# A graph layer on one core: when GpSimd may refill a slot of the ring of gathered rows

## The chip, the core and the metric

The kernel runs on one core of one Trainium2 chip. The metric is the device time of one execution in microseconds (us). TensorE is written PE, VectorE DVE, ScalarE ACT, GpSimd POOL and SyncE SP, as in the profile.

## What is computed

The input is a graph of 2500 nodes with 256 features each and 80000 edges, sorted by destination. The part of the reference that this change touches is the attention over the edges:

```
xl = (xn @ W_l).reshape(N, 4, 64);  xr = (xn @ W_r).reshape(N, 4, 64)
e = xl[src] + xr[dst];  e = where(e >= 0, e, 0.2 * e)
score = einsum('ehd,hd->eh', e, att)
ex = exp(score - segment_max(score, dst)[dst])
agg = segment_sum(ex / segment_sum(ex, dst)[dst] * xl[src], dst)
```

After it come an ELU, a layer norm and a residual, and a sum with a second branch (a lambda layer: a softmax over the nodes, a 256x256 context, a product with queries). Last there is a mixture of eight experts with a capacity, of which each node takes one.

## The kernel before

`graph_block` runs four stages one after the other: `survey` (norms, the tables xl and xr, tables for the edges), `attend` (the attention), `node_update` and `experts`. Only `attend` changes.

The edges are cut into 704 groups of up to 128 edges, and 4 groups make a **quad**: there are `QUADS` = 176 of them. Every engine goes through the quads in the same order with its own instruction stream, and semaphores alone bind the engines together. Eight quads (`RUN`) are a run, since the maxima of the segments are found once for each run. `over_quads` writes the first turn of 16 quads out, then loops nine times over a turn of 16, and writes the last turn out with the steps that follow it. I call the piece of an engine's stream for quad q **its step q**.

- **POOL**, step q: four indirect DMAs at L1080, one for each group. Each fetches 128 rows of `d_xl` (260 floats, 1040 bytes) by source node into `gathered_rows`. This tile is a ring with `RING` = 16 slots of one quad. Slot q % 16 was last used by quad q - 16, so the first two gathers of quad q wait until ACT has made the first half of the products of quad q - 16 (`prod`, two counts for each quad), and the other two wait for the second half. The gathers of quads 0 to 7 are issued by `survey`. Those of quads 8 to 15 stand in the first turn and have nothing to wait for.
- **SP**, step q: loads for quad q into rings of four, `e_drow` (L1014) and `e_xr` (L1015), and the store of the sums (L1030).
- **PE**, step q: `edges(q)`, 12 matmuls that pick rows of xr (L1400), and two that add the gathered rows of groups 0 and 1 by the identity (L1405, 4 in the profile's count); before the first of these PE waits for all four gathers of quad q. The rows of groups 2 and 3 are added by DVE. Behind it in the same stream stands `sums(q - 12)` (L1454), which needs the products of quad q - 12.
- **DVE**, step q: `sum_edges(q)` (L1154), which waits for `edges(q)`, for the gathers of quad q and for an older score; then the mask for quad q + 2 (L1146), two leaky parts (L1160, L1164), the sums of quad q - 13 (L1193), a mask for quad q - 10 (L1179), and `scores(q)` (L1171). In the first five steps of a run there are small operations for the segment maxima too. In the first turn DVE, PE and ACT also do the lambda branch: `keys_less` (L1112), `contexts` (L1346) and others. POOL has one operation of it (L228), behind the gathers of quad 15.
- **ACT**, step q: `weights(q - 11)`, an exponential (L1505) and 16 scaled copies (L1509), the products. It waits for `sums(q - 13)`, which PE does in its step q - 1.

So a gather for quad q is released by products made in ACT's step q - 5, and read by PE and DVE in their step q.

Of the kernel before, what the change touches and what calls it, by code (L numbers as in the profile page):

```python
# [38 lines left out]
RING = 2 * RUN  # L39
# [21 lines left out]
BLANKS = 2 * (TURNS - 2)  # L61
BLANK = -(-(TRASH + 1) // (2 * BLANKS)) * 2
EARLY = RING // 2
LN_EPS = 1e-5
CONSTANTS = 20 * 16


def settle(eng, m):


    eng.sem_inc(m.met, 1)
# [28 lines left out]
def sem_set(nc, ctx, prefix, names):  # L100

    sems = {}
    for name in names.split():
        if name[-1] == "*":
            sems[name[:-1]] = [semaphore(nc, ctx, f"{prefix}_{name[:-1]}{i}") for i in range(2)]
        else:
            sems[name] = semaphore(nc, ctx, f"{prefix}_{name}")
    return sems
# [91 lines left out]
def ring_view(m, half, partitions, *shape, dt=F32):  # L200
# [5 lines left out]
    m.used[half] += n  # L206
    assert m.used[half] <= EARLY * G * ROW
    flat = m.ring[:, half * EARLY * G:(half + 1) * EARLY * G, :].rearrange("p n c -> p (n c)")
    view = flat[0:partitions, at:at + n]
# [16 lines left out]
def rstd_pool(pool, out, var, halves):  # L226

    return pool.tensor_tensor(out, var, halves, ALU.pow)  # L228


def survey(nc, ctx, m, a):
# [104 lines left out]
    with nc.Block() as block:  # L336
# [64 lines left out]
        def _(pool):  # L401
# [10 lines left out]
            def first_rows():  # L412
# [3 lines left out]
                settle(pool, m)  # L416
                for i in range(EARLY * G):
                    pool.indirect_dma_start(m.ring[:, i, :], None, m.d_xl, bass.IndirectOffsetOnAxis(
# [42 lines left out]
        def _(dve):  # L461
            ch = Chain(dve, s["chain"], 0)

            def variances(b):
# [7 lines left out]
                dve.wait_ge(s["norm"], 8 * b + 8)  # L472
                dve.tensor_scalar(ve[:, 4 * b:4 * b + 4], mv[:, 4 * b:4 * b + 4, 1], LN_EPS, None, ALU.add).then_inc(s["var"], 1)

# [451 lines left out]
def over_quads(eng, body, behind=0):  # L926

    for slot in range(RING):
        body(Quad(0, slot))
    with eng.Fori(1, TURNS - 1) as turn:  # L930
        for slot in range(RING):
            body(Quad(turn, slot))
    for slot in range(RING + behind):
        body(Quad(TURNS - 1, slot))


def attend(nc, ctx, m, a):
# [3 lines left out]
    s = sem_set(nc, m.sems, "att", "init idx sel edges summed relu score lin turned run top ends heads fwd bwd carried drop cols raised tops topped diff rr f fac ex prod selt agg old acc rows* links fixed shares")  # L941
# [8 lines left out]
    score = sb("e_score", [P, 2, HEADS, SUBS_RUN])  # L950
# [16 lines left out]
    prod = sb("e_prod", [P, 2, G, HEADS, HCOLS])  # L967
# [35 lines left out]
    with nc.Block() as block:  # L1003
# [61 lines left out]
        @block.gpsimd  # L1065
        def _(pool):
            def quad(q):
                p = q.slot // RUN
                if q.at == 0 and not q.known():
                    pool.wait_ge(s["idx"], q.run - 1)  # L1070
                if q.known() and q.k < EARLY:
                    return
                for g in range(G):
                    if g % 2 == 0 and q.since(RING):
                        pool.wait_ge(s["prod"], (q.k - RING) * 2 + g // 2 + 1)
                    if g % 2 == 0:
                        settle(pool, m)
                    at = q.at * G + g
                    column = m.idx[:, q.k * G + g:q.k * G + g + 1] if q.known() else idx[p][:, at:at + 1]
                    pool.indirect_dma_start(xl[:, q.slot * G + g, :], None, m.d_xl, bass.IndirectOffsetOnAxis(  # L1080
                        ap=column, axis=0)).then_inc(gathered[q.slot], 16)
                if q.known() and q.k == RING - 1:
                    pool.wait_ge(sl["var"], 2)
                    rstd_pool(pool, rs[:, :], ve[:, :], neghalf[:, :]).then_inc(sl["rstd"], 1)
            over_quads(pool, quad)
            pool.wait_ge(sl["mix"], 2)
            pool.tensor_tensor(m.b_mix[:, :], m.b_mix[:, :], m.beta[:, :], ALU.add).then_inc(sl["rowed"], 1)
            pool.wait_ge(sl["rowed"], 1)
            pool.wait_ge(sl["x"], 16 * (FOURS + 1))
            for b in range(FOURS):  # L1090
                four = m.x[:, 4 * b:4 * b + 4, :]
                pool.tensor_tensor(four, four, m.b_mix[:, :].unsqueeze(1).to_broadcast([P, 4, DIM]), ALU.add)

        @block.vector
        def _(dve):
# [23 lines left out]
            def lambda_rows():  # L1119
# [5 lines left out]
                for half in range(2):  # L1125
# [3 lines left out]
                    lamed.step(dve.bn_aggr(mv[:, half, :], st[:, half, :]))  # L1129
                dve.tensor_scalar(ve[:, :], mv[:, :, 1], LN_EPS, None, ALU.add).then_inc(sl["var"], 1)  # L1130

# [427 lines left out]
def node_update(nc, ctx, m, a):  # L1559
# [54 lines left out]
    with nc.Block() as block:  # L1614
# [90 lines left out]
        def _(dve):  # L1705
# [75 lines left out]
            def first_stats(b):  # L1781
# [8 lines left out]
                dve.wait_ge(s["aggr1"], 4 * b + 4)  # L1790
                dve.tensor_scalar(ve1[:, tiles], mv1[:, tiles, 1], LN_EPS, None, ALU.add).then_inc(s["var1"], 1)

            def residual(b):
# [19 lines left out]
                dve.wait_ge(s["aggr2"], 4 * b + 4)  # L1813
                dve.tensor_scalar(ve2[:, tiles], mv2[:, tiles, 1], LN_EPS, None, ALU.add).then_inc(s["var2"], 1)

# [306 lines left out]
```

## Time and profile before

| what | value |
|---|---|
| median of the runs | 1652.13 us |
| lowest, highest of 3 runs | 1651.43, 1689.13 us |
| the profiled execution | 1662.86 us, its span 1661.1 us |
| PE, DVE, ACT, POOL busy, share of the span | 73%, 65%, 51%, 49% |
| granted clock of PE, mean | 0.871 |
| gathers at L1080 | 672 |

The profile is one execution. Its times count from the start of its span; what lies around the span is 1.8 us. The busy time of a POOL gather is the time in which POOL writes it out for the DMA engines, not that of the transfer. "Idle before" is the time in which the engine did nothing ahead of an instruction, and the name behind it what ended it ("remote": an update that the records do not tie to an instruction; "issue": nothing that the profile shows).

### The profile page before, as it was taken

What the parts mean: (1) busy time and instruction counts of PE and PEld (TensorE: products, weight loads), DVE (VectorE), ACT (ScalarE), POOL (GpSimd) and SP (SyncE); (2) the same over time, 40 slices, a digit from 0 to 9 for tenths busy, and PEclk for the clock granted to TensorE, in tenths of its full rate; (3) what the DMA queues carried; (4) which work ended last, traced back from release to release, by engine and by line L of the source; (5) the groups of instructions that cost most, each with busy time, mean ns of one, the idle gap of its engine ahead of it and who ended that gap; (6) DMA issues with size and microseconds to landing.
All of it is one profiled execution on the core that took longest, in us unless ns stands there. A gap on an engine that the chain in (4) does not pass through costs nothing. (4 is left out here: it accounts for less than half of the span.)

```text
span 1661.1 us, 24931 instructions
## 1 busy us (share of the span) xinstructions
PE 1217.6 (73%) x5659; PEld 865.7 (52%) x5659; DVE 1082.3 (65%) x2307; ACT 848.9 (51%) x3252; POOL 816.1 (49%) x849
## 2 busy tenths in 40 slices
PE   6754877767877677777877777867767747399995
PEld 4322755555555555555655555645545536355663
DVE  7442876776776666776778676866767858404444
ACT  3220176656666576657666675756656823132221
POOL 5625055555555555456555565556546154502223
PEclk9866998889898899878889998988989977589997
DMA  6544256555566556566565655656755125334340
GB/s 181 147 150 113 67 142 167 147 161 153 161 169 155 146 159 166 147 166 162 160 161 163 164 164 152 172 151 162 210 147 155 40 65 165 123 120 140 102 127 17
DMA packets 167498, 237.47 MB, mean 143 GB/s; under 512 B 40113, under 2 KB 134018, under 8 KB 167407
## 3 DMA queue, kind: packets, MB, share of 16 engines
q1 hardware_dynamic: 123310, 130.22, 26.9%
q0 software_dynamic: 41216, 103.67, 24.2%
q10 hardware_dynamic: 2880, 2.66, 0.5%
q14 instruction: 72, 0.58, 0.1%
q8 instruction: 20, 0.33, 0.1%
HBM read 189.57 MB, written 48.91 MB: 144 GB/s over the span
## 5 line engine op out<-in xcount | busy, mean ns | idle before, releaser
L1080 POOL DMA_INDIRECT gathered_rows<-d_xl,e_idx x576 | 547.3, 950 | 425.2 <-ACT e_prod L1509 180.6
L1509 ACT ACTIVATE e_prod<-gathered_rows,e_prod 128x64 f32<-128x64 f32 x2728 | 679.1, 335 | 46.4 <-issue 39.6
L1454 PE MATMUL bank<-e_prod,e_selt 128*128 128x260 f32 x1408 | 402.4, 432 | 133.8 <-DMA gathered_rows<-in_src_dram,n_row_of 58.7
L1454 PEld LDWEIGHTS bank<-e_prod,e_selt 128*128 128x128 f32 x1408 | 286.0, 211 | 229.0 <-issue 82.9
L1400 PE MATMUL bank<-e_xr,e_sel 128*128 128x256 bf16 x2112 | 327.2, 293 | 54.0 <-issue 38.5
L1154 DVE TENSOR_TENSOR e_edge<-bank,gathered_rows 128x512 f32<-128x512 f32 x176 | 119.7, 680 | 279.2 <-remote 241.7
L1400 PEld LDWEIGHTS bank<-e_xr,e_sel 128*128 128x128 bf16 x2112 | 217.4, 105 | 154.3 <-issue 81.8
L1405 PE MATMUL bank<-gathered_rows,ident 128*128 128x256 f32 x704 | 233.6, 411 | 36.2 <-issue 36.0
L1171 DVE TENSOR_REDUCE e_score<-e_edge 128x16 f32<-128x1024 f32 x176 | 212.8, 1209 | 0.3
L1505 ACT ACTIVATE e_prod<-e_diff 128x16 f32<-128x16 f32 x176 | 39.4, 224 | 203.6 <-remote 121.6
L1405 PEld LDWEIGHTS bank<-gathered_rows,ident 128*128 128x128 f32 x704 | 118.6, 210 | 39.4 <-issue 33.1
L1080 POOL DMA_INDIRECT gathered_rows<-d_xl,src_cols x96 | 90.7, 945 | 88.1 <-ACT e_prod L1509 29.9
L1179 DVE TENSOR_TENSOR e_selt<-bank,cyclic_cols 128x512 f32<-128x512 f32 x176 | 119.6, 680 | 11.0 <-PE bank L1454 7.2
L1949 POOL DMA_INDIRECT out_dram<-f_out,f_index x32 | 45.3, 1417 | 159.2 <-DVE f_out L2064 154.3
L1160 DVE SCALAR_TENSOR_TENSOR e_edge<-bank,att_relu 128x512 f32<-128x512 f32 x176 | 119.4, 678 | 0.0
L1164 DVE SCALAR_TENSOR_TENSOR e_edge<-e_edge,bank 128x512 f32<-128x512 f32 x176 | 118.5, 673 | 0.0
L1971 PE MATMUL bank<-f_rowst,w_rows 128*128 128x391 f32 x256 | 87.5, 500 | 0.7 <-ACT f_rowst L2012 0.7
L1193 DVE SCALAR_TENSOR_TENSOR e_acc<-e_acc,keep_cols,bank 128x260 f32<-128x260 f32 x154 | 73.4, 476 | 21.4 <-remote 12.5
L1983 PE MATMUL bank<-f_hid,w_rows 128*128 128x391 f32 x256 | 85.8, 492 | 0.0
L1498 ACT ACTIVATE e_rr<-e_drop 1x4 f32<-1x4 f32 x22 | 4.5, 204 | 151.2 <-DVE e_drop L1251 119.1
L1971 PEld LDWEIGHTS bank<-f_rowst,w_rows 128*128 128x128 f32 x256 | 49.3, 193 | 37.4 <-issue 2.7
L1422 PE MATMUL bank<-ident,e_top 128*1 128x128 f32 x22 | 7.1, 322 | 83.7 <-DVE e_top L1221 58.4
(315 smaller groups left out, 1165.0 us busy)
## 6 DMA issues: line engine op xcount, KB each, us to landing
e_xr<-d_xr SPq DMA_DIRECT2D x176, 192.0 KB
d_hist<-e_acc SPq DMA_DIRECT2D x176, 130.0 KB
e_drow<-d_rel SPq DMA_DIRECT2D x176, 128.0 KB
w_rows<-in_L_ffn_w_dram SPq DMA_DIRECT2D x16, 1024.0 KB, 7.2
gathered_rows<-d_xl,e_idx POOLq DMA_INDIRECT x576
d_in<-lambda_w SPq DMA_DIRECT2D x18, 350.7 KB
e_rows<-d_rows SPq DMA_DIRECT2D x22, 192.5 KB
x_rows<-in_x_dram SPq DMA_DIRECT2D x8, 512.0 KB, 5.5
```

What stands on the lines that cost most here:

```text
L1080: pool.indirect_dma_start(xl[:, q.slot * G + g, :], None, m.d_xl, bass.IndirectOffsetOnAxis(ap=column, axis=0)).then_inc(gathered[q.slot], 16)
L1154: dve.tensor_tensor(edge[:, b, 2:4, :], ps_edge[b][1][:, :].rearrange("p (g c) -> p g c", g=2), xl[:, q.slot * G + 2:q.slot * G + 4, 0:DIM ...
L1160: dve.scalar_tensor_tensor(out=edge[:, b, 0:2, :], in0=ps_edge[b][0][:, :].rearrange("p (g c) -> p g c", g=2), scalar=0.0, in1=m.att_relu[ ...
L1164: dve.scalar_tensor_tensor(out=edge[:, b, 2:4, :], in0=edge[:, b, 2:4, :], scalar=0.0, in1=att_relu.unsqueeze(1).to_broadcast([P, 2, DIM]) ...
L1171: dve.tensor_reduce(score[:, p, :, q.at * G:q.at * G + G].rearrange("p h g -> p g h"), edge[:, b, :, :].rearrange("p g (h c) -> p g h c", ...
L1179: dve.tensor_tensor(selt[:, b, :, :], lane_up.unsqueeze(1).to_broadcast([P, G, P]), m.cyclic[:, bass.ds(q.k * G, G)].unsqueeze(2).to_broad ...
L1400: last = pe.matmul(out, sel[:, b, g * P:g * P + P], xr[:, r, part * DIM:part * DIM + DIM], start=(part == 0), stop=(part == 2 and g >= 2))
L1405: last = pe.matmul(out, m.ident[:, :], xl[:, q.slot * G + g, 0:DIM], start=False, stop=True)
L1454: last = pe.matmul(ps_agg[b], selt[:, b, g, :], flat(prod[:, b, g, :, :]), start=(g == 0), stop=(g == G - 1))
L1509: last = act.activation(prod[:, b, g, h, 0:HEAD], xl[:, q.slot * G + g, h * HEAD:h * HEAD + HEAD], ACT.Copy, scale=prod[:, b, g, h, HEAD:H ...
L1971: last = pe.matmul(m.bank[2 + f % 2][:, 0:CAP], w1[:, q, half, f * P:f * P + P], rowst[:, q, half, :], start=(half == 0), stop=(half == 1))
L1983: last = pe.matmul(m.bank[4 + to][:, 0:CAP], w2[:, q, f, to * P:to * P + P], hid[:, f, :], start=(f == 0), stop=(f == FCH - 1))
```

## The change

A constant `LEAD` = 13 is added. From quad 16 on, the gathers of quad q wait for the products of quad q - 13 in place of quad q - 16. In the first turn, the gathers of quads 8 to 15 wait until the scores of quad q - 8 (`EARLY` = 8) are written. Nothing else changes: the ring keeps its 16 slots, and every gather, matmul and load stays.

```diff
+LEAD = 13
...
                 for g in range(G):
                     if g % 2 == 0 and q.since(RING):
-                        pool.wait_ge(s["prod"], (q.k - RING) * 2 + g // 2 + 1)
+                        pool.wait_ge(s["prod"], (q.k - LEAD) * 2 + g // 2 + 1)
+                    elif g == 0:
+                        pool.wait_ge(s["score"], q.k - EARLY + 1)
                     if g % 2 == 0:
                         settle(pool, m)
```

## Rows read from the trace of the kernel before

**Rows 1.** Busy time by stretch: stretch, length, engines, PE clock, DMA share, GB/s

```profile
117.00:162.00 45.00, 18.31 (x77) 11.31 (x77) 11.35 (x20) 2.11 (x2) 30.26 (x32) 0.65 0.43 115
...
211.00:1286.00 1075.00, 796.70 (x4015) 587.41 (x4016) 764.49 (x1468) 681.55 (x2809) 610.99 (x643) 0.89 0.59 160
```

**Rows 2.** Groups by line, DVE from 211 to 1286 us: busy, mean ns, idle before

```profile
L1154 DVE TENSOR_TENSOR e_edge<-bank,gathered_rows 128x512 f32<-128x512 f32 x161 | 109.4, 680 | 240.7 <-remote 212.4 <-PE bank L1405 20.5 <-issue 7.8
```

**Rows 3.** The waits: who for whom, total us, times, longest

```profile
POOL gathered_rows L1080 <- ACT e_prod L1509: 210.5, 79, 10.8
```

**Rows 4.** Timeline of POOL, first turn: start, duration, what, idle before

```profile
117.24 0.94 POOL L1080 DMA_INDIRECT gathered_rows<-d_xl,src_cols  x1 [29.20 <-POOLq L2096]
...
156.00 0.95 POOL L1080 DMA_INDIRECT gathered_rows<-d_xl,src_cols  x1 [0.30 <-issue]
198.97 0.85 POOL L228 TENSOR_TENSOR l_rs<-l_ve,l_neghalf 128x2 f32<-128x2 f32 x1 [42.03 <-DVE l_ve L1130]
210.59 1.02 POOL L1080 DMA_INDIRECT gathered_rows<-d_xl,e_idx  x1 [10.76 <-ACT e_prod L1509]
```

**Rows 5.** Timeline of DVE, quads 0 to 3

```profile
123.86 0.69 DVE L1154 TENSOR_TENSOR e_edge<-bank,gathered_rows 128x512 f32<-128x512 f32 x1 [4.32 <-issue]
...
134.10 0.69 DVE L1154 TENSOR_TENSOR e_edge<-bank,gathered_rows 128x512 f32<-128x512 f32 x1 [5.71 <-remote]
...
162.13 0.69 DVE L1154 TENSOR_TENSOR e_edge<-bank,gathered_rows 128x512 f32<-128x512 f32 x1 [23.49 <-remote]
...
166.58 0.68 DVE L1154 TENSOR_TENSOR e_edge<-bank,gathered_rows 128x512 f32<-128x512 f32 x1
```

**Rows 6.** Timeline of PE, first turn

```profile
138.30 0.28 PE L1400 MATMUL bank<-e_xr,e_sel 128*128 128x256 bf16 x1 [2.22 <-issue]
...
170.08 3.64 PE L1346 MATMUL bank<-xn_rows,x_rows 128*128 128x257 f32 x16
...
175.73 3.64 PE L1346 MATMUL bank<-xn_rows,x_rows 128*128 128x257 f32 x16
```

**Rows 7.** Timeline of POOL: last gather of quads 86 and 88, then quads 89 to 91

```profile
683.65 0.95 POOL L1080 DMA_INDIRECT gathered_rows<-d_xl,e_idx  x1 [0.30 <-issue]
...
700.73 0.95 POOL L1080 DMA_INDIRECT gathered_rows<-d_xl,e_idx  x1 [0.30 <-issue]
704.02 0.94 POOL L1080 DMA_INDIRECT gathered_rows<-d_xl,e_idx  x1 [2.35 <-DMA gathered_rows<-in_src_dram,n_row_of]
...
707.77 0.94 POOL L1080 DMA_INDIRECT gathered_rows<-d_xl,e_idx  x1 [0.30 <-issue]
...
715.27 0.95 POOL L1080 DMA_INDIRECT gathered_rows<-d_xl,e_idx  x1 [0.30 <-issue]
```

**Rows 8.** Timeline of DVE, quads 85 to 87

```profile
707.95 0.68 DVE L1154 TENSOR_TENSOR e_edge<-bank,gathered_rows 128x512 f32<-128x512 f32 x1
...
711.00 1.21 DVE L1171 TENSOR_REDUCE e_score<-e_edge 128x16 f32<-128x1024 f32 x1
718.28 0.69 DVE L1154 TENSOR_TENSOR e_edge<-bank,gathered_rows 128x512 f32<-128x512 f32 x1 [6.07 <-remote]
```

**Rows 9.** Timeline of PE, edges of quad 85 and 86 and what follows

```profile
700.93 0.60 PE L1405 MATMUL bank<-gathered_rows,ident 128*128 128x256 f32 x2
...
704.34 2.02 PE L1454 MATMUL bank<-e_prod,e_selt 128*128 128x260 f32 x8 [0.28 <-issue]
...
707.18 0.60 PE L1405 MATMUL bank<-gathered_rows,ident 128*128 128x256 f32 x2
...
708.42 2.02 PE L1454 MATMUL bank<-e_prod,e_selt 128*128 128x260 f32 x8
```

**Rows 10.** Timeline of ACT, its step 85

```profile
704.19 0.22 ACT L1505 ACTIVATE e_prod<-e_diff 128x16 f32<-128x16 f32 x1
704.44 3.93 ACT L1509 ACTIVATE e_prod<-gathered_rows,e_prod 128x64 f32<-128x64 f32 x16
```

**Rows 11.** The chain that ended last: an indirect DMA of POOL landing

```profile
1649.99 2.19 DMA out_dram<-f_out,f_index
```

## The prediction

> **What bounds the kernel now.** I read the busy time by stretch first. `attend` runs from about 117 to 1345 us, and in its long middle, 211 to 1286 us, DVE is busy for 764.49 of 1075 us, PE for 796.70 and POOL for 610.99 [rows 1]. No engine is full. So I asked for the groups by line: DVE's largest idle time stands before L1154, the first operation of a quad, with 240.7 us for 161 quads, or 1.5 us a quad, and 212.4 of it ends with "remote" [rows 2]. POOL waits for ACT's products for 210.5 us [rows 3].
>
> Then the timelines show what DVE's idle time is. POOL issues gathers 1.25 us apart when nothing holds it (117.24 to 156.00 for 31 steps), 0.95 busy and 0.30 idle [rows 4, 7], 5.0 us for the four of a quad. Where such gathers follow each other for long, the other engines come to a stand. In the first turn 32 of them go out without a break from 117.24 to 156.95 us [rows 4]; DVE starts quad 1 at 134.10 after 5.71 us idle, and quad 2 at 162.13 after 23.49 us [rows 5]. In this time PE issues single matmuls with 2.22 us before one of them, 0.28 us long, and "issue" as the reason [rows 6]: it waits for nothing in the program. In the middle the same is seen on a small scale: 10 gathers from 704.02 to 716.22 [rows 7], and DVE, done with quad 85 at 712.21, starts quad 86 at 718.28, 6.07 us later, though PE had its edges by 708.4, when it began the sums that stand behind them, and though the last gather of quad 86 had been issued at 683.65 [rows 7 to 9]. I call this a **stop**. It begins about 8 us after the start of an unbroken row of gathers and ends about 2 us after the row's end. The path through `attend` is thus DVE's work plus the stops.
>
> The Trainium skill says otherwise ("SBUF — State Buffer", "Who interferes with whom"): a DMA never contends with a compute engine, and "PE and ACT never wait on anyone"; only DVE and GpSimd share ports. The rows of the first turn disagree, with PE standing too. By the page alone, breaking the row of gathers would give nothing, and the forecast would lack its first term.
>
> **The first turn.** The gathers of quads 8 to 15 no longer start at 117.24; those of quad 8 start when the scores of quad 0 are written, those of quad 15 after quad 7. Removed are three idle times of DVE: 4.32 + 5.71 + 23.49 = 33.5 us [rows 5]. They don't all go. The 32 gathers still cost 5.0 us a quad, and quads 2 and 3 follow 4.45 us apart on DVE [rows 5], while PE needs 5.65 us a quad (170.08 to 175.73, with the contexts of the lambda branch) [rows 6]. So POOL has little rest between quads, and stops come here too; but now a stop also holds back the scores that release the next gathers, and ends itself. I price them as in the middle: 8 quads by 1.5 us [rows 2] = 12 us. The gain is 33.5 - 12 = 21.5 us, taken as **20 us**. Bounds: 33.5 us if no stop remains, 0 us if stops follow the number of gathers and not their unbroken row. Eight added waits of POOL cost nothing, since POOL has nothing else: from 156.95 it idles until the one small operation at 198.97, and until 210.59 for its next gather [rows 4]. That small operation of the lambda branch stands behind the gathers of quad 15 in POOL's queue. They would end by about 180 us, before it is wanted, so it is not late.
>
> **From quad 16 on.** The gathers of quad q wait for ACT's step q - 2 in place of q - 5. The cadence does not change by this: ACT still releases four gathers in each step, and what POOL issued at a given time for quad q + 3 it now issues for quad q. What changes is how early the rows are there. I take quads 85 and 86 as the sample. A transfer lands about 2.2 us after its issue ends (the nearest row is another indirect DMA of POOL, 2.19 us) [rows 11]. The gathers at 704.02 to 708.71 [rows 7] would be quad 86's, landed at 710.9; PE came to them at 707.18 [rows 9], so it waits 3.7 us, and with the 1.3 us from there to the edges' end (707.18 to 708.42 in the rows) they are ready at 712.2. DVE is free for quad 86 at 712.21 [rows 8]: nothing lost. The gathers that end at 701.68 [rows 7] would be quad 85's, landed at 703.9; PE came to them at 700.93, 2.9 us earlier [rows 9]. Its next sums began at 704.34 [rows 9] and would begin near 705.2, while DVE took up quad 85 at 707.95 [rows 8]. So PE, which ran ahead of DVE, loses that lead, and DVE has 0 to 2.7 us in hand.
>
> What is queued behind PE's wait are the sums of quad q - 12. ACT's next step needs them: sums that begin near 705.2 and last 2.02 us are done at 707.2, and ACT's step 85 ends at 708.37 [rows 9, 10]. So ACT too has 1.1 us in hand. With both so near to zero, some quads will be late. I take 0.5 us for each run of eight quads, 20 runs, **+10 us**: the sample stands at zero. Bounds: below, -40 us (the second rival's mechanism), since holding ACT back shortens rows of gathers; above, +80 us (the first rival's).
>
> The stretch under gathers also moves three steps later, ACT's steps 14 to 173 in place of 11 to 170. It starts with three steps without stops and ends with three more under them, 3 by 1.5 us each way: zero. SP's queue is not touched, and the gathers, bytes and matmuls are the same, as is everything after `attend`.
>
> The Trainium skill prices the landing in its own way ("DMA: Bandwidth & Descriptors", "Anatomy of one DMA — SWDGE (gpsimd) path"): 2.0 us and the bytes by 436e3 for a microsecond. An estimate from it for 128 rows of 1040 bytes is 2.3 us, beside the 2.19 us of the row; the sum would be the same.
>
> **Sum.** Profiled execution 1662.9 - 20 + 10 = 1652.9 us. It was 10.7 us longer than the median of the runs, so against the median: 1652.1 - 20 + 10 = **1642 us**.
>
> **Rivals.** (1) *PE's wait paces everything* (slower). PE waits for the gathers ahead of the sums, ACT waits for the sums, POOL for ACT. Where quads now follow each other in ACT's 4.2 us (704.19 to 708.37) [rows 10], they would follow in POOL's 5.0: 0.8 us by 5 quads of a run by 20 runs = 80 us, so 1652 - 20 + 80 = 1712 us. It decides once PE's lateness passes what ACT and DVE have in hand, 1.1 and 2.7 us; 3.7 us at quad 86 speaks for it. Against it: the middle takes 6.7 us a quad (1075 / 161) [rows 1, 2], so on the mean POOL has time to catch up, and the stops hide lateness, as at quad 86.
>
> (2) *The wait breaks up the rows of gathers* (faster). When PE waits, ACT makes products later, and the 10 gathers in a row become 8 or fewer. If one stop of each run loses 2 us, 20 runs give 40: 1652 - 20 - 40 = 1592 us. For it: the stops, 212.4 us, are the largest loss there is. Against it: the same 5.0 us of issue for each quad must be placed in the same time.
>
> (3) *Stops follow the number of gathers*, so that the change does nothing in the first turn, and the lateness remains: 1652 + 10 = 1662 us. Against it: the 23.49 us stand just at the one row of 32.
>
> **How the numbers follow.** Forecast 0.50, rival 1 0.18, rival 2 0.18, rival 3 0.14. The forecast's own range is 1620 to 1665 us, rival 3 included. The whole range goes from 1595 to 1705: it takes in most of rival 2 and the milder half of rival 1. Two per cent, about what a measurement of this kernel can tell from no change, is 33 us: under 1619 lie rival 2 and the edge of the forecast, 0.20; above 1685 rival 1, 0.18; between them 0.62.
>
> **What would show it.** In the new profile DVE's L1154 for quad 2 should start near 135 to 140 us and the 32 gathers should stand in groups of four to eight; quad 16 should start some 20 us earlier than now. PE's L1405 should have idle time before it with a DMA as its reason, 1 to 4 us in many quads, and DVE's idle time before L1154 in the middle should stay near 1.5 us a quad. I am wrong if DVE's mean idle time there moves by more than 0.3 us a quad either way (48 us), or if quad 2 still waits for the last of the 32 gathers.

## The result: slower by 3.7%

The changed kernel takes 1714.06 us, median of four runs (1713.11 to 1714.24); the kernel before took 1655.11 us, median of four runs beside it. The ratio is 1.037, 95% interval 1.032 to 1.042. The profiled execution has a span of 1712.2 us, before it was 1661.1. The forecast was 1642 us, and the time lies above its whole range, 1595 to 1705; 1712 us was the price of the first rival.

All lines after the new constant stand three lines lower: L1154 is now L1157, L1405 is L1408, L1509 is L1512.

Busy time by stretch, kernel after (stretch, length, PE, PEld, DVE, ACT, POOL, granted clock, DMA share, GB/s), beside [rows 1]:

```profile
117.00:162.00 45.00, 37.55 (x199) 29.70 (x200) 30.11 (x47) 5.87 (x6) 21.41 (x23) 0.91 0.46 117
211.00:1286.00 1075.00, 756.75 (x3773) 567.57 (x3773) 719.27 (x1377) 638.13 (x2647) 573.55 (x606) 0.86 0.57 152
```

From 117 to 162 us, in the first turn, DVE does 47 operations where it did 20. In the long middle every engine does less in the same time: POOL issues 606 instructions in place of 643.

Starts of quads on DVE, kernel after: quads 0 to 3, then 16, then 160:

```profile
122.64 0.69 DVE L1157 TENSOR_TENSOR e_edge<-bank,gathered_rows 128x512 f32<-128x512 f32 x1 [3.66 <-PE bank L1408]
127.08 0.68 DVE L1157 TENSOR_TENSOR e_edge<-bank,gathered_rows 128x512 f32<-128x512 f32 x1
131.52 0.68 DVE L1157 TENSOR_TENSOR e_edge<-bank,gathered_rows 128x512 f32<-128x512 f32 x1
138.93 0.69 DVE L1157 TENSOR_TENSOR e_edge<-bank,gathered_rows 128x512 f32<-128x512 f32 x1 [2.89 <-remote]
...
224.72 0.69 DVE L1157 TENSOR_TENSOR e_edge<-bank,gathered_rows 128x512 f32<-128x512 f32 x1
...
1251.78 0.68 DVE L1157 TENSOR_TENSOR e_edge<-bank,gathered_rows 128x512 f32<-128x512 f32 x1
```

The same in the kernel before, quads 16 and 160, and one group of its middle that the prediction had not looked at:

```profile
243.38 0.69 DVE L1154 TENSOR_TENSOR e_edge<-bank,gathered_rows 128x512 f32<-128x512 f32 x1 [2.77 <-remote]
...
1204.10 0.69 DVE L1154 TENSOR_TENSOR e_edge<-bank,gathered_rows 128x512 f32<-128x512 f32 x1
```

```profile
L1256 DVE COPY e_cols<-bank 128x2 f32<-128x2 f32 x20 | 3.0, 152 | 2.5 <-PE bank L1429 2.4
```

This splits the result in two. Quad 16 starts 18.7 us earlier (224.72 for 243.38). From quad 16 to 160 the kernel before needs 960.7 us, the changed one 1027.1: 66.4 us more, 0.46 us a quad or 3.7 us a run of eight. The first gain is real, and the second part eats it more than three times over.

Where the 66 us are: DVE's groups in the middle (211 to 1286 us), kernel after, beside [rows 2]:

```profile
L1157 DVE TENSOR_TENSOR e_edge<-bank,gathered_rows 128x512 f32<-128x512 f32 x150 | 102.1, 680 | 258.2 <-remote 173.0 <-PE bank L1408 82.0 <-issue 3.2
...
L1259 DVE COPY e_cols<-bank 128x2 f32<-128x2 f32 x19 | 3.0, 158 | 30.8 <-PE bank L1432 21.9 <-issue 8.9
```

and the waits of the same stretch, beside [rows 3]:

```profile
POOL gathered_rows L1083 <- ACT e_prod L1512: 305.2, 84, 24.7
DVE e_edge L1157 <- remote: 173.0, 31, 8.7
...
PE bank L1408 <- DMA gathered_rows<-d_xl,e_idx: 155.8, 50, 6.5
ACT e_prod L1508 <- DVE e_diff L1273: 95.4, 15, 8.3
```

The last of them in the kernel before:

```profile
ACT e_prod L1505 <- DVE e_diff L1270: 11.9, 8, 2.1
```

"Remote" before the first operation of a quad is down from 212.4 to 173.0 us, while "PE bank", the edges, is up from 20.5 to 82.0. PE, which in this stretch of the kernel before never waited for gathered rows, now waits 50 times, 155.8 us in all. POOL waits longer for products (305.2 for 210.5), and ACT for `e_diff` (95.4 for 11.9): the scores less the maximum of their segment, which DVE makes once a run and without which ACT can't begin the run's products. So less time goes in stops, and in its place stands a wait through the whole ring: POOL for ACT, PE for POOL's rows, DVE for PE, ACT for DVE. The idle time before the first operation of a quad grew only from 1.50 to 1.72 us a quad (258.2 / 150), half of the loss; another part, 30.8 us for 2.5, stands at L1259, once a run, behind PE's L1432. L1432 is queued behind the edges of the run's third quad.

The loss isn't spread evenly over a run. By place in the run (means of the 18 runs from quad 16 to 160, starts on DVE), the way from the fifth quad to the sixth takes 11.36 us where it took 7.63, the one from the second to the third 8.96 where it took 6.47, and the next 7.02 for 5.32. The ways to the fifth and to the seventh quad are shorter than before, by 2.1 and 2.7 us.

PE also runs slower where it has to wait (set 3 shows it), but here that is little: between quads 16 and 160 its granted clock is 0.88 before and 0.86 after, and its busy time 4.97 and 5.02 us a quad.

### The profile page after: what moved, and what is told of

It reads as the page before. It is cut to its first block and busy times, and to the rows that moved or that the text cites. A ratio compares the mean times of both kernels' runs of the same rounds, so it can differ in the third digit from the quotient of the medians.

```text
span 1712.2 us, 24931 instructions
## 1 busy us (share of the span) xinstructions
PE 1225.1 (72%) x5659; PEld 882.7 (52%) x5659; DVE 1082.7 (63%) x2307; ACT 845.1 (49%) x3252; POOL 814.2 (48%) x849
## 5 line engine op out<-in xcount | busy, mean ns | idle before, releaser
L1512 ACT ACTIVATE e_prod<-gathered_rows,e_prod 128x64 f32<-128x64 f32 x2728 | 675.0, 334 | 34.4 <-issue 28.4
L1408 PE MATMUL bank<-gathered_rows,ident 128*128 128x256 f32 x704 | 257.4, 453 | 232.9 <-DMA gathered_rows<-d_xl,e_idx 155.8
L1457 PEld LDWEIGHTS bank<-e_prod,e_selt 128*128 128x128 f32 x1408 | 303.7, 221 | 122.5 <-issue 51.2
L1403 PE MATMUL bank<-e_xr,e_sel 128*128 128x256 bf16 x2112 | 311.7, 286 | 19.4 <-DVE e_sel L1149 8.8
L1157 DVE TENSOR_TENSOR e_edge<-bank,gathered_rows 128x512 f32<-128x512 f32 x176 | 119.9, 681 | 297.5 <-remote 195.5
L1403 PEld LDWEIGHTS bank<-e_xr,e_sel 128*128 128x128 bf16 x2112 | 212.6, 102 | 104.7 <-issue 35.7
L1408 PEld LDWEIGHTS bank<-gathered_rows,ident 128*128 128x128 f32 x704 | 122.9, 219 | 262.2 <-DMA gathered_rows<-d_xl,e_idx 172.2
L1952 POOL DMA_INDIRECT out_dram<-f_out,f_index x32 | 45.3, 1415 | 160.4 <-DVE f_out L2067 155.6
L1986 PEld LDWEIGHTS bank<-f_hid,w_rows 128*128 128x128 f32 x256 | 47.9, 189 | 33.6
## 6 DMA issues: line engine op xcount, KB each, us to landing
d_in<-lambda_w SPq DMA_DIRECT2D x18, 350.7 KB
```

The source lines that it names most:

```text
L1157: dve.tensor_tensor(edge[:, b, 2:4, :], ps_edge[b][1][:, :].rearrange("p (g c) -> p g c", g=2), xl[:, q.slot * G + 2:q.slot * G + 4, 0:DIM ...
L1403: last = pe.matmul(out, sel[:, b, g * P:g * P + P], xr[:, r, part * DIM:part * DIM + DIM], start=(part == 0), stop=(part == 2 and g >= 2))
L1408: last = pe.matmul(out, m.ident[:, :], xl[:, q.slot * G + g, 0:DIM], start=False, stop=True)
L1457: last = pe.matmul(ps_agg[b], selt[:, b, g, :], flat(prod[:, b, g, :, :]), start=(g == 0), stop=(g == G - 1))
L1512: last = act.activation(prod[:, b, g, h, 0:HEAD], xl[:, q.slot * G + g, h * HEAD:h * HEAD + HEAD], ACT.Copy, scale=prod[:, b, g, h, HEAD:H ...
L1986: last = pe.matmul(m.bank[4 + to][:, 0:CAP], w2[:, q, f, to * P:to * P + P], hid[:, f, :], start=(f == 0), stop=(f == FCH - 1))
```

## The experiments

Sixteen runs were made, in four sets; inside a set all stand beside the same runs of the kernel before. One fact is needed to read them: the kernel before took 1667 us in the first and the fourth set, near the 1655 us of the result, but 1335 us in the second and the third. The kernel is the same; the stops of the prediction are there in the first case and missing in the second (last section). So ratios are compared only inside a set. I call the two cases the ground with stops and the ground without. Diffs are against the changed kernel.

**Set 1, with stops (before 1667.1 us): the two halves of the change, and the length of the lead.**

`first_turn_only` keeps the wait on the scores and puts the other back to sixteen:

```diff
-LEAD = 13
+LEAD = 16
```

> LEAD is 16 again, and only the wait on the scores in the first turn stays. Theory A (the first turn gains, the shorter lead costs): quad 16 starts near 225 us as in the changed kernel, not at 243 as before, the middle goes at the 6.7 us a quad of before, and the time is 15 to 20 us under before, 1635 to 1640 us. Theory B (spreading the gathers only moves the stops to later quads): the gain at quad 16 is gone by quad 160, and the time is that of before within 4 us.

1650.0 us, ratio 0.992 (0.988 to 0.996). Quad 3 starts at 144.4 us and quad 16 at 230.3; from there to quad 160 it is 6.70 us a quad, as before the change (6.67). Theory A holds, though the absolute time was expected 10 to 15 us lower.

`lead13_only` leaves out the two lines of the first-turn wait:

```diff
-                    elif g == 0:
-                        pool.wait_ge(s["score"], q.k - EARLY + 1)
```

> The first turn is that of before (32 gathers in a row), and LEAD is 13. Theory A: DVE's 23 us stop is back, the middle goes at 7.1 us a quad, and the time is 60 to 75 us over before, 1715 to 1730 us. Theory B: the loss needs both parts, and this one alone costs under 30 us.

1731.9 us, ratio 1.041 (1.037 to 1.046). Quad 2 again starts at 160.4 us, after the 32 gathers, and the middle takes 7.08 us a quad (7.13 with both halves). The two halves are separate, and the whole loss belongs to the thirteen: theory A again.

`lead14`, first-turn wait kept:

```diff
-LEAD = 13
+LEAD = 14
```

> Both parts, with LEAD 14. Theory A says that the loss is lateness of the gathered rows at PE: one step more of lead is 6.7 us, more than the 1 to 4 us by which PE was late, so nearly all of the loss goes: 1635 to 1645 us. Theory C (waiting for younger products makes ACT, POOL and PE run in a tighter ring, whatever the lateness): a third of the loss stays away at most, 1680 to 1695 us.

1650.8 us, ratio 0.989 (0.986 to 0.993): 6.72 us a quad. All of the loss is gone, as theory A has it.

`lead12`, likewise:

```diff
-LEAD = 13
+LEAD = 12
```

> Both parts, with LEAD 12. Theory A: PE is now late by some 8 us at nearly every quad, and DVE's few microseconds in hand are gone, so the loss grows far more than by another third: over 1790 us. Theory C: one third more, 1735 to 1745 us.

1954.3 us, ratio 1.174 (1.169 to 1.178): 8.6 us a quad, far over the 1790 us that theory A gave as the least. The timeline of the kernel with 12, PE's edges of two quads, two apart, and POOL before the second:

```profile
709.26 1.22 PE L1408 MATMUL bank<-gathered_rows,ident 128*128 128x256 f32 x2 [7.19 <-DMA gathered_rows<-d_xl,e_idx]
...
728.03 1.22 PE L1408 MATMUL bank<-gathered_rows,ident 128*128 128x256 f32 x2 [8.13 <-DMA gathered_rows<-d_xl,e_idx]
...
721.45 0.94 POOL L1083 DMA_INDIRECT gathered_rows<-d_xl,e_idx  x1 [8.55 <-ACT e_prod L1512]
```

Every second quad PE stands for POOL's rows, and POOL stands for ACT, which stands for PE. From 16 to 14 the lead costs nothing, then 4% and 17%: a cliff, not a slope. With 14, PE's idle time before L1408 is 49.3 us over the kernel, 40.6 of it "issue"; with 13 it is 232.9, 155.8 of it the wait for these gathers. So with 14 the rows are nearly always there when PE comes to them (8.5 us of waits for them in all), and with 13 often not.

**Set 2, without stops (before 1335.3 us): is it PE's wait standing ahead of the sums, or POOL's issuing?**

`lead13_sums_first` splits PE's step. The edges that need gathered rows (groups 0 and 1) go behind the sums of quad q - 12; `lead16_sums_first` is its control with sixteen:

```diff
-                    edges(q)
+                    edges(q, (2, 3))
...
+                if q.exists():
+                    edges(q, (0, 1))
```

> As the changed kernel, but in PE's step the two matmuls of gathered rows (and the part of the edges behind the first of them) come after the sums, so PE no longer holds the sums back while it waits for the gathers. Theory P (the order in PE's stream makes the loss, since the sums wait behind the gathers): ACT is no longer late, and the loss of the middle falls to under 20 us: 1640 to 1660 us. Theory Q (the ring ACT, gather, PE's edges, DVE is too long by itself, 5.0 us of issue for each quad in it): the loss stays, 1700 us or more.

> The control of the run before: the same order in PE's step with LEAD 16. The edges now wait for ACT's products too, which may cost DVE something. Both theories: within 15 us of the kernel with LEAD 16 and the wait of the first turn, 1640 to 1665 us.

1469.4 us, ratio 1.098 (1.092 to 1.105), and for the control 1387.2, 1.038 (1.034 to 1.043). So the order alone costs 52 us, where at most 15 were expected, and thirteen in this order another 82. In the third set, on the same ground, thirteen in the old order costs 245 us. Neither theory is right alone: with the sums out of the way thirteen costs a third of what it did, but 82 us remain. The control is itself 52 us slower, which may hide some of the lateness, so the pair doesn't price the order exactly; against the kernel before, the run with thirteen is 134 us slower.

`half_lead16` and `half_lead13` issue only the gathers of groups 0 and 1 from quad 16 on, with the waits on them halved, so that groups 2 and 3 of each quad are computed from old rows and the output isn't the reference's:

```diff
+                    if q.since(RING) and g >= 2:
+                        continue
```

> From quad 16 on only the gathers of groups 0 and 1 are issued; groups 2 and 3 use what the ring held, so the output is not the reference's. LEAD is 16, and the wait of the first turn stays. POOL issues 2.5 us a quad. If the stops come from long unbroken rows of gathers, rows of 4 remain at most, the stops go, and with them some 190 of DVE's 212 us of remote waits: 1440 to 1480 us. If they have another cause, 1600 us or more.

> The same half of the gathers with LEAD 13. If the loss is POOL's 5.0 us of issue in a short ring, half of it makes the ring 2.5 us shorter, and the time is within 10 us of the same with LEAD 16. If waiting for younger products costs by itself, it stays 50 us or more above.

1299.2 us, ratio 0.973 (0.967 to 0.979) and 1405.1 us, 1.052 (1.046 to 1.059); two executions each. The first expectation had the ground with stops in mind and missed by 140 us or more: where there are no stops there is little for half the gathers to take away. The pair still says something. With half the issuing (2.5 us a quad) thirteen costs 106 us against its control, where the full kernel loses 245. The expectation put a loss of 50 us or more down to waiting for younger products as such. So it isn't only POOL's 5.0 us a quad that paces the ring, as rival 1 had it.

**Set 3, without stops (before 1334.9 us): which quads.**

`changed_again` is the changed kernel itself.

> The changed kernel again, as the base of this set: the kernel before took 1667 us in the set with the other leads, but 1335 us in the set with the split edges, where rows of 28 to 32 unbroken gathers stopped nobody. Where the kernel before takes about 1655 to 1667 us, 3.5% more; where it takes about 1335 us, the missing stops leave the short ring bare, and I expect 8 to 12% more, 1440 to 1490 us.

1579.6 us, ratio 1.185 (1.179 to 1.190): on this ground the loss is 245 us, well over the 8 to 12% expected. The first-turn wait was not run alone here, but `narrow_lead16` below has it, with whole rows up to quad 15, and takes the time of the kernel before. In this set the trace of the changed kernel shows the path without stops on it. Timelines of its quad 93, the sixth of its run, in the order of the path (DVE's e_diff, ACT's step 91, POOL's gathers, PE, DVE):

```profile
669.20 0.27 DVE L1273 TENSOR_TENSOR e_diff<-e_score,bank 128x128 f32<-128x128 f32 x1
...
669.58 0.23 ACT L1508 ACTIVATE e_prod<-e_diff 128x16 f32<-128x16 f32 x1 [5.81 <-DVE e_diff L1273]
669.85 3.93 ACT L1512 ACTIVATE e_prod<-gathered_rows,e_prod 128x64 f32<-128x64 f32 x16
...
672.65 0.94 POOL L1083 DMA_INDIRECT gathered_rows<-d_xl,e_idx  x1 [4.70 <-ACT e_prod L1512]
...
676.39 0.95 POOL L1083 DMA_INDIRECT gathered_rows<-d_xl,e_idx  x1 [0.30 <-issue]
...
675.69 1.15 PE L1403 MATMUL bank<-e_xr,e_sel 128*128 128x256 bf16 x9
681.47 0.71 PE L1408 MATMUL bank<-gathered_rows,ident 128*128 128x256 f32 x2 [4.63 <-DMA gathered_rows<-d_xl,e_idx]
...
683.71 0.69 DVE L1157 TENSOR_TENSOR e_edge<-bank,gathered_rows 128x512 f32<-128x512 f32 x1 [4.35 <-PE bank L1408]
```

A run's first products can't be made before e_diff. ACT has stood for 5.81 us for it. The first products release quad 93's first gathers 3.1 us later; the fourth is issued at 677.34; the rows are there at 681.47, 4.1 us after that; the edges are done at 683.5. From e_diff to DVE's quad 93 it is 14.2 us (683.71 - 669.47), and in them DVE had only quads 91 and 92 to do, some 4.4 us each. The missing 4.35 us are its idle time. In `narrow_lead16`, with sixteen and without stops, the same way takes 9.8 us.

The same kernel, quad 90, the third of its run: POOL's last gather, PE, and what is queued behind it:

```profile
651.48 0.95 POOL L1083 DMA_INDIRECT gathered_rows<-d_xl,e_idx  x1 [0.30 <-issue]
...
660.71 0.70 PE L1408 MATMUL bank<-gathered_rows,ident 128*128 128x256 f32 x2 [4.13 <-DMA gathered_rows<-d_xl,e_idx]
...
665.54 0.28 PE L1432 MATMUL bank<-ident,e_carried 1*128 1x1 f32 x2
...
665.86 0.16 DVE L1259 COPY e_cols<-bank 128x2 f32<-128x2 f32 x1 [2.47 <-PE bank L1432]
```

Here the rows arrive 8.3 us after the issue ended. PE's L1432, on which the same e_diff depends, stands behind the late edges and the sums. So one late quad makes e_diff late, e_diff makes the first products late, and these the gathers of the sixth quad.

The third quad isn't late by chance. Wherever PE waits for it, its rows come 7.8 us after the last issue (median of 18 runs; 4.9 us for the sixth quad, 3.7 for the first), and in the trace of the result 7.6 us (12 runs). Once a run, while these gathers are being issued, SP issues a load of 350.7 KB (`d_in<-lambda_w` in the profile, here at 649.9 us), and from 655 to 661 us the DMA engines are busy for 0.84 of the time, against 0.62 in the mean of quads 16 to 160. That this load delays the rows is argued, not shown.

PE's wait has a second price. PE's sums behind the late edges of quad 90 and those of the step after it, timeline and busy time by stretch (columns as above):

```profile
662.45 3.16 PE L1457 MATMUL bank<-e_prod,e_selt 128*128 128x260 f32 x8
...
668.05 1.92 PE L1457 MATMUL bank<-e_prod,e_selt 128*128 128x260 f32 x8
```

```profile
661.00:665.50 4.50, 4.50 (x15) 3.32 (x14) 0.69 (x1) 2.77 (x12) 1.88 (x2) 0.62 0.35 78
666.00:672.00 6.00, 6.00 (x41) 4.83 (x38) 5.96 (x14) 2.39 (x10) 1.65 (x2) 1.00 0.45 131
```

After 4.13 us of waiting PE's granted clock is 0.62 of full speed for these 4.5 us, most of them at the lower of its two levels, 1.2 GHz; then it is 1.00 again, 2.4 GHz. The same eight matmuls take 3.16 us in place of 1.92. PE is busy 4.83 us a quad here and 4.41 in `narrow_lead16` (clock 0.88 and 0.97), 0.42 of the 1.57 us by which a quad is longer. How much of that lies on the path was not tested.

`lead13_free5` gives the sixth quad of each run its old lead, and `lead16_only5` shortens the lead of that quad alone:

```diff
-                        pool.wait_ge(s["prod"], (q.k - LEAD) * 2 + g // 2 + 1)
+                        pool.wait_ge(s["prod"], (q.k - (RING if q.at == 5 else LEAD)) * 2 + g // 2 + 1)
```

> The changed kernel, but the gathers of the sixth quad of each run (q % 8 = 5) wait for quad q - 16 again. Theory R: the loss sits at this quad, since its gathers are released by the first products of a run, and these wait for the segment maxima that DVE finishes two steps of its own before it needs the rows. Then at least half of the loss against the kernel before goes. Theory S: the loss is spread over all quads at which PE is late: an eighth of it goes.

> The mirror image: every quad waits for quad q - 16, only the sixth of each run for quad q - 13. POOL issues in order, so the quads behind it are late with it. Theory R: at least half of the loss of the changed kernel is here. Theory S: less than a fifth.

1523.9 us, ratio 1.141 (1.137 to 1.144), and 1495.8 us, 1.123 (1.118 to 1.129). One quad in eight with the short lead costs 161 us, two thirds of the 245; freeing the same quad gives back only 56, less than the half that theory R asked for. The costs don't add. With the sixth quad free, DVE's idle time before it falls to 0.1 us a run, and before the seventh, where the lateness then shows, it is 3.0. The wait in `lead16_only5` is the one of above, timelines of ACT, POOL, PE and DVE:

```profile
577.15 0.23 ACT L1508 ACTIVATE e_prod<-e_diff 128x16 f32<-128x16 f32 x1 [6.75 <-DVE e_diff L1273]
...
580.23 0.95 POOL L1083 DMA_INDIRECT gathered_rows<-d_xl,e_idx  x1 [9.64 <-ACT e_prod L1512]
...
590.23 1.22 PE L1408 MATMUL bank<-gathered_rows,ident 128*128 128x256 f32 x2 [5.83 <-DMA gathered_rows<-d_xl,e_idx]
...
592.98 0.69 DVE L1157 TENSOR_TENSOR e_edge<-bank,gathered_rows 128x512 f32<-128x512 f32 x1 [5.99 <-PE bank L1408]
```

POOL stood for 9.64 us at the wait of this one quad, and the gathers of the later quads, which stand behind it in POOL's stream, stood with it.

`narrow_lead16` was to show whether stops follow bytes: from quad 16 on each gather moves 65 of the 260 floats of a row, and of other rows, so that its output isn't the reference's.

```diff
-                    pool.indirect_dma_start(xl[:, q.slot * G + g, :], None, m.d_xl, bass.IndirectOffsetOnAxis(
+                    pool.indirect_dma_start(xl[:, q.slot * G + g, 0:WIDE if q.since(RING) else ROW], None,
+                                            narrow if q.since(RING) else m.d_xl, bass.IndirectOffsetOnAxis(
```

> LEAD 16 and the wait of the first turn; from quad 16 on each gather fetches 65 floats a row in place of 260, and from other rows, so the output is not the reference's. The number of gathers is the same, the bytes are a quarter. If the stops come from POOL's writing out of the gathers, they stay, and the time is within 30 us of the same kernel with whole rows; if they come from the bytes in flight, they go, and the time falls by 100 us or more where the kernel before takes 1655 us. Where it takes 1335 us there is nothing to tell.

1334.5 us, ratio 1.000 (0.997 to 1.002). On a ground without stops it can't answer; inconclusive.

**Set 4, with stops (before 1666.7 us): repairs, and the better versions again.**

`lead13_free25` frees the third quad too (`q.at in (2, 5)`); `free5_sums_first` frees the sixth and has PE's order of set 2; `first_turn_again` and `lead14_again` are kernels of set 1.

> The changed kernel, but the gathers of the third and of the sixth quad of each run wait for quad q - 16. Theory R (the run's turn from one to the next is what is late: the third quad's gathers land 8 us after their issue, the sixth quad's are released by the run's first products): half or more of the loss goes. Theory P (the loss is that PE holds the sums back whenever it waits, at any quad): the lateness moves to the quads beside them, as it did when the sixth alone was freed, and a third or less goes.

> LEAD 13 with both repairs, the sixth quad freed and PE's sums ahead of the gathered rows. With the sums first alone, the loss against its own control with LEAD 16 was 82 us. If order and sixth quad are the whole cause, it falls below 25 us: under 1412 us where the kernel before takes 1335 us. If something third is there, it stays above 50 us.

> LEAD 16 and the wait of the first turn alone. Where the kernel before takes 1655 to 1667 us it gains 13 us again. Where it takes 1335 us, no row of gathers stops anybody, so the wait has nothing to gain and nothing to lose: within 3 us of the kernel before.

> Both parts with LEAD 14. Where the kernel before takes 1335 us a quad takes 5.0 us and not 6.7, so a step of lead is worth less and LEAD 14 is as tight as 13 is on the slower ground: a loss of 2 to 6%, 1360 to 1415 us. Where it takes 1655 us: 1% faster, as in its first run.

The ratios are 1.026 (1.021 to 1.031), 1.020 (1.013 to 1.027), 0.990 (0.987 to 0.994) and 0.992 (0.988 to 0.996). The changed kernel has no run in this set; with the 1.037 of the result, the repairs take back a quarter and two fifths of the 4.5% that lie between it and the first turn alone. For `lead13_free25` that is theory P (a third or less), as far as numbers of two sets can be compared. For `free5_sums_first` the expectation named times for the other ground only, and it decides nothing. Neither reaches the first turn alone: six quads of eight, or seven, still have the short lead. How much of the second one's rest is the order itself isn't known, since its control ran only without stops. The fastest versions are the first-turn wait with a lead of 16 or of 14, 13 to 18 us under the kernel before by the ratios, seen in two sets; no interval reaches 1. For `lead14_again` the expectation with stops was met; without stops fourteen was never run, and it was expected to cost 2 to 6% there.

## Why the prediction was wrong

**The first turn: right.** Forecast 20 us; quad 16 starts 18.7 us earlier, and the kernel with this part alone gains 13 and 16 us in two sets (0.8% and 1.0% of 1667). That the idle times go but not wholly was right as well. In the trace after, gathers go out in rows of 12, 4, 12 and 4, not of four to eight as forecast, and three stops of 2.9 to 8.1 us remain, before quads 3, 4 and 7. The prediction's rule that a stop ends about 2 us after its row fits the row of 10 it was read from; the one before quad 2 ended 5.2 us after the row of 32. Rival 3 (stops follow the number of gathers) is out. By the Trainium skill ("SBUF — State Buffer", "Who interferes with whom"), where a DMA never contends with a compute engine, breaking the row should have given nothing. The 18.7 us weren't to be had by that rule alone; but the page is about ports of SBUF, and no run here shows where in the chip a stop arises. On the ground without stops I have no run of the first turn alone.

**The shorter lead: wrong, and this is the step that failed:** "I take 0.5 us for each run of eight quads, 20 runs, +10 us: the sample stands at zero." Measured from quad 16 to 160: 3.7 us a run. Three things stand behind it, in the order of what the runs show.

First, *the loop through e_diff was left out.* Quads 85 and 86 are the sixth and the seventh of their run, so the sample held the very quad whose gathers, with thirteen, hang on the run's first products. The prediction gave them the times at which POOL had issued three quads later, kept everything else in its place, and found 2.7 us in hand for DVE at quad 85. It followed PE → sums → ACT → POOL and left out DVE → e_diff → ACT → POOL → PE → DVE. And what it had in hand came from a stop. Timeline of DVE in the kernel before, e_diff of the run and quad 84:

```profile
693.53 0.27 DVE L1270 TENSOR_TENSOR e_diff<-e_score,bank 128x128 f32<-128x128 f32 x1
...
703.43 0.69 DVE L1154 TENSOR_TENSOR e_edge<-bank,gathered_rows 128x512 f32<-128x512 f32 x1 [4.25 <-remote]
```

From the end of e_diff to quad 85 it is 14.1 us (693.81 to 707.95), 4.25 of them the stop before quad 84. The loop that `changed_again` shows is as long, 14.2 us, and where no such stop stands in it DVE waits. In the result's own trace ACT waits 95.4 us for e_diff, 11.9 before, and the way to the sixth quad is the one that grew most. The loop isn't seen bare there: of DVE's 6.3 us of idle time before the sixth quad (mean of 18 runs; 2.4 before the change) most ends with "remote", so stops stand on top of it. `lead16_only5` prices this quad alone at 161 us on its ground, where the whole costs 245.

Second, *the landing was misread and mis-sized.* I took 2.19 us behind the issue's end from another indirect DMA, at the quiet end of the kernel [rows 11]. But that piece of the chain starts with the issue, as POOL's timeline of the kernel before shows:

```profile
1649.99 1.20 POOL L1949 DMA_INDIRECT out_dram<-f_out,f_index  x1 [0.30 <-issue]
```

So it is 2.19 us from the issue's start and 1.0 from its end. The page of `changed_again` has the median for these gathers, from the issue's start to landing:

```profile
gathered_rows<-d_xl,e_idx POOLq DMA_INDIRECT x576, 4.0
```

That is 3.0 us from the end, 0.8 more than I took. By the prediction's own sums it leaves ACT 0.3 of its 1.1 us at quad 85, and DVE is 0.8 us late at quad 86. Where PE had to wait, the rows came later still: 3.3 us after the last issue in the trace of the result (median of 55 waits from quad 16 on, 1.8 to 8.0 us), which uses up the 1.1 us. The Trainium skill's formula ("DMA: Bandwidth & Descriptors", "Anatomy of one DMA — SWDGE (gpsimd) path") gives an estimate of 2.3 us for such a gather; that is near the 2.19 us at the end of the kernel and far under the 4.0 us of the loaded middle.

Third, *the slacks were treated as separate.* `lead13_sums_first` takes PE's wait out of the sums' way and cuts the loss from 245 to 82 us against its control; `lead13_free5` takes out e_diff's loop and cuts 56. Neither takes all of it, and when the sixth quad is freed the seventh is late. I don't have a kernel that removes both with a control on one ground, so how the 245 us divide stays open, and so does the part of PE's lower clock and of the third quad's late rows.

**Rival 1: right time, partly for its reason.** Its price was POOL's 5.0 for ACT's 4.2 us, 0.8 us by five quads. The time came out at 1712 forecast, 1714 measured. PE's lateness did pass the 1.1 us, as it said, and ACT's waits for PE's sums went from 45.9 to 84.8 us in the middle. But the loss doesn't have its form: it isn't 0.8 us at five quads of a run but 3.7 us at the sixth and 2.5 and 1.7 at the third and the fourth, with gains between them, and with half the gathers the thirteen still cost 106 us (`half_lead13` against `half_lead16`). The agreement of the size is largely luck.

**Rival 2: stops lessened, but not by its mechanism.** "Remote" before L1157 fell from 212.4 to 173.0 us. But the rows of gathers were not broken up: from quad 16 to 160, counting a break as more than 0.45 us, there are 105 rows of 5.5 gathers in the mean before, 8 of them of ten or more, and 101 rows of 5.7 after, 9 of ten or more. Why less time goes in stops is not shown, and what took its place was larger.

**The sign to look for: too narrow.** I said I would be wrong if DVE's idle time before the first operation of a quad moved by more than 0.3 us a quad. It moved by 0.22, and yet the quads take 0.46 us more: the mean hid gains and losses at different quads, and the rest stands before L1259 and other lines once a run. PE's waits, 50 of 3.1 us in the mean, were in the range given (1 to 4 us), and "quad 2 near 135 to 140" came as 131.5.

## What to carry to other kernels

When a ring's lead is cut, find the longest stall that comes once a period (here the run's first products after e_diff), and follow from it every dependence that the shorter lead closes, until it comes back to the engine that caused it. Ask of each slack in the sample what made it: here it was smaller than a stop that stood in front of it. Price the landing of a transfer from the same kind of transfer under the same load, and see whether a row counts from the issue's start or its end. And try the neighbouring values: 14 costs nothing and 13 costs 4%, so a lead that is free at one value says little of the next.

## What was not expected of the hardware

The kernel before took 1655 to 1667 us in three comparisons and 1335 us in two, whatever ran beside it. In the faster ones, rows of gathers without a break longer than 0.45 us stop nobody. Timeline of the kernel with sixteen and the sums first (second set): POOL's gathers where a longer wait comes between, and DVE:

```profile
576.25 0.94 POOL L1083 DMA_INDIRECT gathered_rows<-d_xl,e_idx  x1 [1.39 <-ACT e_prod L1516]
...
618.89 0.94 POOL L1083 DMA_INDIRECT gathered_rows<-d_xl,e_idx  x1 [2.81 <-ACT e_prod L1516]
...
583.94 0.69 DVE L1157 TENSOR_TENSOR e_edge<-bank,gathered_rows 128x512 f32<-128x512 f32 x1 [4.55 <-PE bank L1409]
588.38 0.69 DVE L1157 TENSOR_TENSOR e_edge<-bank,gathered_rows 128x512 f32<-128x512 f32 x1
...
597.08 0.67 DVE L1157 TENSOR_TENSOR e_edge<-bank,gathered_rows 128x512 f32<-128x512 f32 x1
601.25 0.68 DVE L1157 TENSOR_TENSOR e_edge<-bank,gathered_rows 128x512 f32<-128x512 f32 x1
```

From the first of these waits to the second 32 gathers go out, and DVE takes up a quad every 4.2 to 4.5 us beside them without one "remote". In `narrow_lead16`, whose gathers are short, all of them from quad 16 to 160 form one row without such a break, and DVE's idle time before a quad is 0.11 us in the mean. On the other ground ten gathers in a row cost DVE 6.07 us [rows 8] and 32 cost it 23.49 [rows 5]. What makes the difference, and what a stop is, no run here shows; the record has the same chip, number 7, for set 1 with stops and set 2 without, so it isn't the chip alone. That narrower gathers would avoid stops could only be tried where there were none. It matters for the reading, since a lead of thirteen costs 65 us with stops (`lead13_only`) and 245 us without (`changed_again`). That stops hide lateness, because all engines stand while transfers land, would fit that; it is argued, not shown.
